# The scan's carry factors: from TensorE products and ScalarE exponentials to a DRAM scratch tensor read back by DMA

## The reference

```
x = silu(conv(h @ Wx.T));  b = x @ Wb.T;  c = x @ Wc.T      # 8 heads, state 64, head size 64
dt = softplus(x @ Wdt.T + b_dt);  a = -exp(log_a)
state = exp(dt * a) * state + (dt * b) outer x              # per head, 64 x 64
y     = c . state
```

## Time and profile before

| | |
|---|---|
| median of 3 runs | 1469.33 us (1468.57 to 1469.62) |
| profiled execution | 1468.33 us, span 1466.3 us |
| TensorE busy | 1372.3 us, 94% of the span |
| VectorE busy | 996.5 us, 68% |
| ScalarE busy | 689.5 us, 47% |
| GpSimd busy | 308.7 us, 21% |
| DMA | 54.24 MB, mean 37 GB/s |

### The profile page before, as it was taken

How to read it: one execution, slowest core, us unless ns; L and a number is a source line. 1 busy time by engine, 2 the same in 40 slices (tenths; PEclk the granted TensorE clock), 3 DMA queues, 4 the chain that set the end, 5 groups by cost and what they waited for, 6 DMA issues and landing times.

```text
span 1466.3 us, 23175 instructions
## 1 busy us (share of the span) xinstructions
PE 1372.3 (94%) x8656; PEld 849.5 (58%) x8656; DVE 996.5 (68%) x2848; ACT 689.5 (47%) x1353; POOL 308.7 (21%) x386
## 2 busy tenths in 40 slices
PE   7999999999999999999999999999999999998434
PEld 2447655676457665576456764576655764567423
DVE  2426797477874787477974778747874779747782
ACT  4434543645445462635436454555626354362212
POOL 3004201241104301142013411043011420133110
PEclk9999999999999999999999999999999999999767
DMA  8001001020000200020010200001000200101010
GB/s 302 6 0 30 15 15 47 3 75 29 25 23 10 68 30 26 22 77 15 15 47 3 76 30 26 22 20 59 29 26 22 77 15 15 47 4 45 29 47 4
DMA packets 47534, 54.24 MB, mean 37 GB/s; under 512 B 7608, under 2 KB 42296, under 8 KB 47424
## 3 DMA queue, kind: packets, MB, share of 16 engines
q1 hardware_dynamic: 41408, 46.42, 9.4%
q0 software_dynamic: 6016, 6.35, 1.7%
HBM read 34.84 MB, written 17.87 MB: 36 GB/s over the span
## 4 chain that ended last, share of the span: by engine, by line
PE 87%; DVE 6%; issue 3%; ACT 1%; DMA 1%; POOL 1%; POOLq 0%; SPq 0%; DVEq 0%; ACTq 0%
PE ps L1519 43%; PE ps L1684 8%; PE ps L1634 5%; PE ps L1593 4%; PE ps L1586 4%; DVE yst L1130 3%; PE ps L1646 2%; PE ps L1605 2%; PE ps L1824 2%; PE ps L1834 2%; PE ps L1620 2%; PE ps L1624 1%; PE ps L1611 1%; PE ps L1789 1%; PE ps L1755 1%
## 5 line engine op out<-in xcount | busy, mean ns | idle before, releaser
L1519 PE MATMUL ps<-xT,wb_s 128*128 128x512 f32 x512 | 230.9, 597 | 0.1
L1519 PE MATMUL ps<-xT,wc_s 128*128 128x512 f32 x512 | 225.4, 593 | 0.0
L1519 PEld LDWEIGHTS ps<-xT,wc_s 128*128 128x128 f32 x512 | 96.1, 190 | 112.3 <-issue 111.9
L1519 PEld LDWEIGHTS ps<-xT,wb_s 128*128 128x128 f32 x512 | 93.6, 190 | 108.4 <-issue 100.9
L1011 DVE SCALAR_TENSOR_TENSOR xT<-xc,cols_s,xT 128x512 f32<-128x512 f32 x192 | 134.8, 748 | 3.2 <-ACT xT L697 0.6
L1519 PE MATMUL ps<-hT,wx_s 128*128 128x512 f32 x256 | 119.0, 609 | 1.9 <-ACT hT L662 1.5
L1684 PE MATMUL ps<-CT,xT 128*128 128x256 f32 x512 | 114.0, 384 | 6.3 <-DVE xT L1190 6.3
L1519 PE MATMUL ps<-hT,wz_s 128*128 128x512 f32 x256 | 112.3, 592 | 0.0
L1684 PEld LDWEIGHTS ps<-CT,xT 128*128 128x128 f32 x512 | 98.7, 193 | 23.2 <-issue 9.8
L729 ACT ACTIVATE BT<-ps 128x512 f32<-128x512 f32 x64 | 37.9, 593 | 151.2 <-PE ps L1519 151.2
L770 ACT ACTIVATE XB<-ps 128x512 f32<-128x512 f32 x64 | 38.4, 599 | 138.3 <-PE ps L1605 138.3
(11 more groups left out here) (298 smaller groups left out, 2589.0 us busy)
## 6 DMA issues: line engine op xcount, KB each, us to landing
BT<-x SPq DMA_DIRECT2D x8, 1024.0 KB, 5.5
xr<-x SPq DMA_DIRECT2D x8, 1024.0 KB, 9.2
x_scratch<-xr SPq DMA_DIRECT2D x32, 256.0 KB, 2.1
out<-EC SPq DMA_DIRECT2D x32, 256.0 KB, 2.1
modrow<-mod_scratch SPq DMA_DIRECT2D x8, 512.0 KB, 6.8
w_s<-w SPq DMA_DIRECT2D x2, 1024.0 KB, 12.4
xT<-wmod SPq DMA_DIRECT2D x1, 1024.0 KB, 8.6
wb_s<-wbT SPq DMA_DIRECT2D x1, 1024.0 KB, 10.6
```

The costliest lines, as they stand in the source:

```text
L1519: ins = t_.matmul(bank[:, :], w[:, k, m * P:(m + 1) * P], rhs[:, k, half * HALF:(half + 1) * HALF], start=k == 0, stop=k == nk - 1)
```

## The change

The products with `spread`, their eight PSUM jobs and the eight exponentials per batch go. In their place:

- VectorE also writes da in the order (head, chunk) into `dah`.
- TensorE makes a second product from it, `dah` as weights (64 columns) against `upto`: 64 rows (head, chunk) x 128 tokens of cum, in the same PSUM bank.
- VectorE copies it to `ev`, ScalarE takes one exponential of 64 x 128 (`carry_factors`, ahead of `w_exp`).
- SP stores `ev` (32 KB) to the DRAM tensor `carry_scratch`, and reads it back with four DMAs of 512 KB, each filling the 64 partitions of one head half with the rows of four heads, for one half of the tokens. They wait for the store, and until the attention of the batch before has read `EC` (the job `F_AV`).
- GpSimd's `carry` waits for these loads.

`carries(b)` stands ahead of `prefetch(b)` and `loads(b)` on SP; for batch 0 and 7 ahead of `loads`. The exponential is taken of the f32 sums. Three set-up instructions for `spread` on GpSimd go with it.

```diff
-SP_ALL = 46
+SP_ALL = 43
+        e_d = nc.dram_tensor("carry_scratch", (T * HEADS, P), F32, kind="Internal").ap()
-        spread = sb("spread", [P, P], BF16)
+        ev = sb("ev", [T * HEADS, P])
+        dah = xc[:, 3072:3136]
-        proj = ring("proj", ps[0:4], 49)
+        proj = ring("proj", ps[0:4], 41)
...
+            def carries(b):
+                sp.wait_ge(carry_ready, at(carry_ready, b, 1))
+                if later(b):
+                    for half in range(2):
+                        sp.wait_ge(carry_loaded[half], at(carry_loaded[half], b - 1, 32))
+                sp.dma_start(e_d[:, :], ev[:, :]).then_inc(carry_stored, 16)
+                if later(b):
+                    sp.wait_ge(*ffn.full(b - 1, F_AV))
+                else:
+                    sp.wait_ge(setup_dve, SD_MIX)
+                sp.wait_ge(carry_stored, at(carry_stored, b, 16))
+                rows = e_d.rearrange("(k s c) n -> s k (c n)", k=NG, s=2)
+                for half in range(2):
+                    for hh in range(2):
+                        sp.dma_start(ECv[64 * hh:64 * hh + 64, :, half * HALF:(half + 1) * HALF],
+                                     rows[hh, :, half * HALF:(half + 1) * HALF].partition_broadcast(64)
+                                     ).then_inc(carry_loaded[half], 16)
...
             def carry(b, half):
-                pool.wait_ge(*proj.read(b, J_EC + 4 * half + 3))
+                pool.wait_ge(carry_loaded[half], at(carry_loaded[half], b, 32))
...
+            def carry_factors(b):
+                act.wait_ge(cumT_ready, at(cumT_ready, b, 1))
+                a.activation(ev[:, :], ev[:, :], ACT.Exp).then_inc(carry_ready, 1)
-            def ec(b, half):
-                for k in range(KC):
-                    q = J_EC + half * KC + k
-                    act.wait_ge(*proj.full(b, q))
-                    a.activation(ECv[:, k, half * HALF:(half + 1) * HALF], proj.bank(q)[:, :], ACT.Exp
-                                 ).then_inc(proj.drained[q % 4], 1)
...
             def decay_steps(b):
-                v.tensor_tensor(da.rearrange(...), dtt.rearrange(...), arow..., ALU.mult).then_inc(da_ready, 1)
+                chD(dve, b, v.tensor_tensor(da.rearrange(...), dtt.rearrange(...), arow..., ALU.mult))
+                v.tensor_copy(dah.rearrange("p (h c) -> p h c", c=T), da.rearrange("p (c h) -> p h c", c=T)
+                              ).then_inc(da_ready, 1)
             def decay_parts(b):
                 dve.wait_ge(*proj.full(b, J_CUM))
+                if later(b):
+                    dve.wait_ge(carry_stored, at(carry_stored, b - 1, 16))
+                v.tensor_copy(ev[:, :], proj.bank(J_CUM)[0:T * HEADS, P:2 * P]).then_inc(cumT_ready, 1)
...
                 t_.matmul(bank[:, 0:64], upto[:, :], da, start=True, stop=True)
+                t_.matmul(bank[0:T * HEADS, P:2 * P], dah, upto[:, :], start=True, stop=True)
-            def carry_rows(b, half):
-                pe.wait_ge(*proj.read(b, J_R))
-                for k in range(KC):
-                    q = J_EC + half * KC + k
-                    pe.wait_ge(*proj.read(b, q - 4))
-                    t_.matmul(proj.bank(q)[:, :], spread[:, :], R8[:, k, half * HALF:(half + 1) * HALF],
-                              start=True, stop=True).then_inc(proj.filled[q % 4], 1)
```

More of the change, by code:

```diff
@@ L44 @@
 SD_MOD, SD_MIX, SD_ALL = 10, 12, 16
-SP_ALL = 46
+SP_ALL = 43
 DT_FLOOR = 2.0 ** -60
-CHAINS = {"A": 4, "V": 9, "D": 7, "S": 4, "G": 20, "R": 45}
+CHAINS = {"A": 4, "V": 9, "D": 8, "S": 4, "G": 20, "R": 45}
 PER_BATCH = {}
@@ L284, in adaln_block @@
         x_loaded = sig("x_loaded", 16)
+        cumT_ready = sig("cumT_ready")
+        carry_ready = sig("carry_factors_ready")
+        carry_stored = sig("carry_factors_stored", 16)
+        carry_loaded = [sig(f"carry_factors_loaded{half}", 32) for half in range(2)]
         xr_loaded = sig("xr_loaded", 16)
@@ L446, in _ @@
             for b in range(1, NB - 1):
+                carries(b)
                 prefetch(b)
@@ L449, in _ @@
                 stores(b)
+            carries(NB - 1)
             loads(NB - 1)
@@ L510, in _ @@
                                  pattern=[[-1, NG], [-NG, 32]], channel_multiplier=1))
-            halves = spread[:, :].rearrange("p (s n) -> p s n", s=2)
-            link(g.memset(spread[:, :], 1.0))
-            link(g.affine_select(out=halves, in_=halves, compare_op=ALU.is_ge, fill=0.0, base=-ROWS,
-                                 pattern=[[-64, 2], [0, 64]], channel_multiplier=1))
-            link(g.affine_select(out=halves, in_=halves, compare_op=ALU.is_ge, fill=0.0, base=2 * ROWS - 1,
-                                 pattern=[[64, 2], [0, 64]], channel_multiplier=-1))
             for src, value, first in ((Lsrc, 1.0, ROWS), (Rsrc, -1.0, 0)):
@@ L893, in batch @@
                     ffn_AT(f)
+                carry_factors(b)
                 w_exp(b)
@@ L901, in batch @@
                     ffn_hnbT(f)
-                ec(b, 0)
                 if f is not None:
                     ffn_gelu(f)
-                ec(b, 1)
                 scan(b, last)
```

10 lines of the change are left out of this document (5 added, 5 removed).

## The result

| | median us | executions | ratio to before |
|---|---|---|---|
| before | 1469.61 (1467.50 to 1475.39) | 19 | |
| after | 1472.70 (1470.69 to 1475.38) | 19 | 1.0017 [1.0010, 1.0024] |

The changed kernel is 0.17% slower, where 0.11% faster was forecast. It lies 0.7 us above the range. By the bound of 0.2% the two are the same, but the interval leaves a ratio of 1 out. The profiled execution took 1472.78, span 1470.8 (before: 1466.3).

The account below looks back on a forecast made before the run. TensorE, busy 94%, was taken to bound the kernel, with ScalarE's path as long to within 0.15 us. -3.93 + 0 + 2.3 = -1.6 us gave 1466.7 profiled, 1467.7 as median; range 1464.5 to 1472.0.

Parts of the forecast that it names:

- Products of batches 1 to 7: TensorE's products around the FFN: 12.0 us of work goes, ScalarE's copy and gelu are late next, so 0.
- The bound of -12.0: Most that removing 14 groups of products, 0.86 us each, in batches 1 to 7 could save.
- Batch 0: No FFN stands between; scores no longer wait behind 3.93 us of ScalarE exponentials: -3.93, once.
- the size of the extra product in the decay sums: One more TensorE product per batch, on the path: 0.29 each, 8 x 0.29 = +2.3; ends +1.4 and +4.6.
- Table load, VectorE, ScalarE: Exponential's table load runs ahead of its wait; VectorE's copies, bank release and ScalarE's small exponential are covered: 0 each.
- Factor loads: Four 512 KB loads, at most 9.2 us; halves in at about 271 and 275.2, before GpSimd needs them: 0.
- no term for the tail's clock: The sum had no tail clock term; the forecast's own range allowed 0.5 us of scatter.
- The base: Starting point: median shown 1469.33, 1.0 above the profiled execution's 1468.33; added to 1466.7 it gave 1467.7.
- Rival D: Clock falls because TensorE gets two new idle gaps a batch, 0.7 to 0.8 us each; chance 2%.
- Rivals A: Freed ScalarE brings its copy and gelu forward; TensorE gains up to 12.0 us: 1455.7; chance 8%.
- B: Table load lands on the scan's start, L759 1.28 later, +9.0 over seven batches: 1476.7; chance 4%.
- C: Factors' second half comes late in batch 0, GpSimd waits, +7.5: 1475.2; chance 4%.

Follow-up runs that it names:

- the last experiments: Transposes ahead of the last projection, gelu awaited by halves: kernel before 1471.03; changed kernel with extra product moved 1455.65, with 48 tail filler products too 1446.24.
- The pad on the kernel before: Kernel before with two small products more (64 columns, 0.22 us each) in the last batch's decay sums: 1471.72, ratio 1.0008.
- the filled kernel: Changed kernel, extra product moved, 48 filler products in the tail, scan's scores and decay differences put ahead of the two FFN products: 1460.27, ratio 0.9941.

## Why the prediction was wrong

The error is 5.0 us: 1472.7 against 1467.7.

*Products of batches 1 to 7: right.* 0 was taken, the kernels with products and exponentials left out, and without the extra product, show 170.75 against 170.76. The two distances behind L1741 and L1840 came as forecast, 1.12 and 0.78. The bound of -12.0 was real too, as the last experiments show (13.6 us): the time was there, behind two waits. The two new idle places, 0.74 and 0.78 us, left the clock alone: it stayed full through 1334.6 us with both in every batch from the second on.

*Batch 0: right.* -3.93 forecast, -3.8 measured.

*The first step that failed: the size of the extra product in the decay sums.* It was sized at 0.29, by a group of eight passes in a row, with 0.58 as the upper end. It measured 0.50 a batch, 0.45 where it stands and 0.05 behind it: 8 x 0.21 = 1.7 us of the error. The single product between others did not reach the pace of the long group; why was not tested. That nothing stood behind it to cover it was read rightly: moved by 13 us, it cost 0.00.

*Table load, VectorE, ScalarE: right.* The load stands ahead of the wait (at 279.23, the exponential at 285.04). The bank's release cost nothing (170.75 a batch without the product, 170.76 in the kernel before).

*Factor loads: the price was wrong, the 0 right.* All four were to be in within 9.2 us, the first half at about 271 and the second by 275.2. One load has a median of 8.9 us to landing, but all four of the second batch took 13.9 from the first issue to the last landing, the halves being in at 273.5 and 279.0. GpSimd takes up the second only at 291.12, so 12 us of slack covered the error.

*The second step that failed, and the larger: no term for the tail's clock.* The tail was left as it was because no edit touches it, and the scatter was put at half a microsecond. Shown is:

- The tail of the kernel before took 182.67 us in one profile and 186.36 in another, 3.7 apart, with nothing changed.
- The kernel before has a mean clock of 0.975 or more in 84 of 120 executions, the changed one in 0 of 30. There are more than two courses: the eight executions of the kernel before at 0.971 took 1475.4 to 1476.3, longer than any that was profiled.
- Which course is taken goes with the moment at which the tail's work comes, to 0.2 us in the five profiles compared above. 0.44 us added made one kernel 2.5 us faster and took another from 84 of 120 executions at 0.975 or more to 3 of 12.

The changed kernel comes 0.1 late from the batches and 0.2 more by VectorE's pause, and against the clock its profiles show the 0.2 alone. In the two profiles its tail has 10.2 us more at half clock and takes 2.6 us more. Of the 2.5 us between the medians (1472.66 - 1470.19 in table 2) 0.3 are its own. The pad on the kernel before costs 1.5, some 1 of it by the clock, and the other 1.2 is put down to the clock by what the profiles show, not by an experiment. That the difference vanishes when TensorE's idle time in the tail is filled (1468.51, 1468.49) says that the rest lies there too, within the 1 to 2 us of those intervals.

*The base.* The median of three runs was 1469.33, of 120 it is 1470.19: 0.9 us of the error was in the starting point, which is luck of the draw. Together 0.9 + 1.7 + 2.4 = 5.0; the 2.4 is what is left, 0.2 for the pause and 2.2 that is laid to the clock.

Rival D had the clock falling in the batches; the clock's part was real, but in the tail, and 2.2 us are laid to it. Rivals A, B and C did not come about (1.12 behind L1741; the load ahead of the wait; no wait at 291.12). That the clock falls only in the tail is not what the trace says: in the kernel before it is also at half for 3.41 us at 19.18. That the range was missed by only 0.7 us is no merit: it had no room for the 3.7 us by which the kernel before differs from itself.

## What to carry to other kernels

Removing work from a busy engine gains only what no wait behind it takes back: here two groups of products of 0.86 us a batch went, and the batch came from 170.76 to 170.75. Look up how far the next engine's chain is from being late, and take those waits away in the same change: 0 became 13.6 us by a new order around the two waits. Put an added instruction where its engine waits anyway: the extra product cost 0.50 us a batch at its first place and 0.00 there. And with a difference under 0.3%, look first at how the unchanged part of the kernel differs between executions of the same program: here its tail by 3.7 us, 0.25% of the whole.

## Of the hardware, not expected

The clock fell once in a stretch that is otherwise busy, with only short waits ahead: in the filled kernel, behind waits of 0.56 and 1.35 us in one batch of seven, the clock was at half for one stretch (the batch took 1.50 us more), though the same waits left it full in the others. One case does not show that the waits did it. The windows view there, and TensorE's line inside it:

```profile
1133.00:1136.00 3.00, 1.17 (x9) 0.86 (x8) 2.56 (x8) 0.57 (x1) 0.19 (x1) 1.00 0.00 0
1136.00:1139.30 3.30, 3.22 (x12) 1.96 (x12) 2.35 (x4) 0.62 (x2) 2.62 (x1) 0.50 0.00 0
```

```profile
1136.08 1.12 PE L1628 MATMUL ps<-ident,xT 128*128 128x128 f32 x4 [1.35 <-ACT XB L789]
```

VectorE's pause of 0.2 us stands at a line that the change leaves alone, and is gone when the extra product is moved (which gives VectorE one more wait in each batch). What it is stays open; no instruction stands in it.
